# The weight and table preparation of a two-stage transformer kernel moved into its first attention stage

## What is computed

```python
dist = jnp.clip(seq[None, :] - seq[:, None], -MAX_POS, MAX_POS) + MAX_POS
attn = jax.nn.softmax(dots + conv[:, dist][None], axis=-1)
```

## Time and profile before

| | us |
|---|---|
| median of 3 runs (lowest, highest) | 3166.3 (3165.73, 3174.5) |
| the profiled execution: its own time | 3165.4 |
| its span, first to last instruction | 3163.4 |
| PE busy, share of the span | 2896.4, 92% |
| DVE busy | 2419.2, 76% |
| ACT busy | 2144.4, 68% |
| POOL busy | 380.2, 12% |

### The profile page before, as it was taken

How to read it: one execution, slowest core, us unless ns; L and a number is a source line. 1 busy time by engine, 2 the same in 40 slices (tenths; PEclk the granted TensorE clock), 3 DMA queues, 4 the chain that set the end, 5 groups by cost and what they waited for, 6 DMA issues and landing times. The chain is left out here.

```text
span 3163.4 us, 49154 instructions
## 1 busy us (share of the span) xinstructions
PE 2896.4 (92%) x19007; PEld 1293.5 (41%) x19007; DVE 2419.2 (76%) x3075; ACT 2144.4 (68%) x2683; POOL 380.2 (12%) x322
## 2 busy tenths in 40 slices
PE   5699999999779999999999999999999999999994
PEld 4356656665433333333333333333333333333331
DVE  6655656565868888888888888888888888888843
ACT  1155656555447777777777777777777777777783
POOL 0000000000001111111101111111111110111114
PEclk9699999999979999999999999999999999999996
DMA  6000000004244434435444444443453544345202
GB/s 178 18 11 2 28 2 22 8 23 82 59 94 77 104 93 88 111 93 111 75 100 95 94 104 99 86 97 94 88 110 97 107 74 105 95 88 110 53 22 88
DMA packets 144399, 243.90 MB, mean 77 GB/s; under 512 B 56562, under 2 KB 92934, under 8 KB 140838
## 3 DMA queue, kind: packets, MB, share of 16 engines
q1 hardware_dynamic: 143590, 238.67, 34.0%
q10 hardware_dynamic: 576, 2.10, 0.2%
HBM read 163.82 MB, written 74.10 MB: 75 GB/s over the span
## 5 line engine op out<-in xcount | busy, mean ns | idle before, releaser
L1598 ACT ACTIVATE pt_b<-ps_max 128x1024 f32<-128x1024 f32 x1516 | 1491.7, 1025 | 364.5 <-PE ps_max L1469 360.5
L1623 DVE TENSOR_REDUCE mx_b<-ps_pair 128x2 f32<-128x1024 f32 (+1 forms) x989 | 1193.5, 1207 | 166.9 <-PE ps_pair L1455 158.7
L1504 PE MATMUL ps_ctx<-pt_b,vs 128*32 128x512 f32 x6144 | 820.6, 606 | 3.8 <-ACT c_b L1587 3.5
L1623 DVE TENSOR_REDUCE mx_b<-ps_misc 128x1 f32<-128x512 f32 x989 | 677.7, 685 | 144.0 <-PE ps_misc L1455 125.7
L1469 PE MATMUL ps_max<-qs,ks 50*128 50x512 f32 x3032 | 780.4, 436 | 1.3 <-ACT part L1555 0.9
L1455 PE MATMUL ps_pair<-ks,qs 48*128 48x512 f32 x1955 | 512.3, 458 | 84.8 <-DVE mx_b L1623 84.6
L1469 PEld LDWEIGHTS ps_max<-qs,ks 50*128 50x128 f32 x3032 | 353.2, 186 | 344.0 <-ACT pt_b L1598 254.0
L1455 PE MATMUL ps_misc<-ks,qs 48*128 48x512 f32 x989 | 441.8, 447 | 7.1 <-DVE mx_b L1623 0.3
L960 ACT ACTIVATE pt<-ps_max,cb 128x512 f32<-128x512 f32 x340 | 215.0, 686 | 223.3 <-PE ps_max L801 159.5
L1455 PEld LDWEIGHTS ps_pair<-ks,qs 48*128 48x128 f32 x1955 | 207.4, 184 | 364.8 <-DVE mx_b L1623 332.5
L1455 PEld LDWEIGHTS ps_misc<-ks,qs 48*128 48x128 f32 x989 | 183.2, 185 | 333.4 <-DVE mx_b L1623 260.7
(11 more groups left out here) (194 smaller groups left out, 2257.6 us busy)
## 6 DMA issues: line engine op xcount, KB each, us to landing
partd<-part SPq DMA_DIRECT2D x22, 2048.0 KB, 9.1
qs<-partd SPq DMA_DIRECT2D x288, 128.0 KB, 5.6
ks<-partd SPq DMA_DIRECT2D x288, 128.0 KB, 6.7
xv<-node SPq DMA_DIRECT2D x26, 512.0 KB, 5.5
xf<-node SPq DMA_DIRECT2D x24, 512.0 KB, 4.7
node<-nt_b SPq DMA_DIRECT2D x48, 256.0 KB, 2.1
rec_b<-invd SPq DMA_DIRECT2D x368, 32.0 KB, 1.8
xq<-node SPq DMA_DIRECT2D x22, 512.0 KB, 3.8
```

What stands on the lines that cost most here:

```text
L1504: ins = pe.matmul(psO[SLOT * i:SLOT * i + SLOT, :], vs[u % 2][:, kb, QUAD * (s // HALF_STEPS) + i], pt[:, (QUAD * S + i) % ENTRIES], start ...
L1598: act.activation(pt[:, e:e + 2].rearrange("p k n -> p (k n)"), at[:], ACT.Exp, scale=SCALE_B).then_inc(exp_done, 1)
L1623: nc.vector.tensor_reduce(mx2[:, at:at + n], (psP, psX)[p % 2][:, 0:CHUNK * n].rearrange("p (h n) -> p h n", h=n), AX.X, ALU.max).then_inc ...
```

## The change

The block `prelude` and the HBM tensor `xnt` are gone, and their work stands in `first_attention`.

- **Tables.** `ext` has six rows: high parts for scores (0, 1) and maxima (2, 3), low parts for scores (4, 5), split by DVE on the 8 partitions of `extended()` before they are written. 32 DMAs read them straight into `tabM` and `tabS`. The products with `flip` are gone: `eye`, the stationary matrix of the window products, is built from the exchange matrix instead of the identity. The eight DMAs for the maxima of heads 0 to 3 go first, the other 24 after the loads of the fold's weights.
- **Layer norm.** Batch 0 is loaded to `xu`, normalised there (`next_stats`, `next_norm`) and turned into `xnb`. Batch b+1 is loaded during batch b, with statistics at step 4 of half 2b, `root_next` at step 6, the norm at step 8, and four transpositions each at steps 10 and 12 (`rows_turned`, `next_turned`). Loading it waits for the earlier rows to be turned.
- **Fold.** PE's part is cut in 13 pieces that follow the maxima p = 4, 6, ..., 28 of half 0; the copies and scalings run on ACT instead of DVE. All its tiles lie in storage that half 0 needs later (`pt`, `cn`, `c32`, `vs[1]`, `x1`, `nt`, `rec`, `den`), so ACT waits for `w_out_s` (results landed in HBM) before the first exponential. The three result DMAs are issued ahead of `rows_load(1)` and of the first `mr<-mhl`.
- **Setup.** Memsets move from DVE to POOL, the constants `cm` from before the projections to after the last maximum of half 0; `wo` and `bo` are waited for only before the first score.

The diff, cut to its core:

```diff
-    xnt = dram("xnt", [BATCH, P, TOK])
...
-    ext = dram("ext", [4, HEADS, NE])
+    ext = dram("ext", [EXT_ROWS, HEADS, NE])
...
-def prelude(nc, psM, psS, psX, sid, exchange, x_rows, conv, conv_rev, ew, act_w, We, be, Wq, Wk, Wv, Wo, ident,
...
+        weights = [within(cn[:], 4 * P * c, [4, P]) for c in range(4)] + [within(c32[:], 4 * P * c, [4, P]) for c in range(2)]
...
+        wos = within(vs[1][:], 0, [NODES, P])
+        wps, wvs, wfs = (within(pt[:], at, shape) for at, shape in (
+            (0, [NODES, WP_COLS]), (NODES * WP_COLS, [NODES, P]), (NODES * (WP_COLS + P), [NODES, WF_COLS])))
...
+        dv_ = within(pt[:], 0, [2, NE])[0:HEADS]
+        de = [within(pt[:], 2 * NE * (k + 1), [2, NE])[0:HEADS] for k in range(2)]
+        dhi = within(units.ks[1][:], 0, [4, NE])[0:HEADS]
+        dlo = within(units.qs[1][:], 0, [2, NE])[0:HEADS]
...
+                sp.dma_start(cv[:, 1], conv).then_inc(cv_in, D16)
+                sp.dma_start(cv[:, 0], conv_rev).then_inc(cv_in, D16)
+                sp.dma_start(xu[:], x_rows[0]).then_inc(xs_in, D16)
+                sp.dma_start(sid[:], ident).then_inc(id_in, D16)
+                sp.dma_start(exch, exchange).then_inc(id_in, D16)
                 sp.dma_start(wqk[:], w_qk).then_inc(w_in, D16)
...
+                                src = bass.AP(ext.tensor, ((2 + s) * HEADS + QUAD * q + odd) * NE + first + DQK * (1 - b),
+                                              [[1, DQK], [2 * NE, 2], [1, WIN]])
+                                sp.dma_start(tabM[rows, q, s, b].bitcast(F32), src).then_inc((tab_first, tab_in)[q], D16)
+
+                sp.wait_ge(ext_high, 1)
+                ext_write(dhi[:, 2:4].bitcast(F32), 2, ext_m_out)
...
+                sp.wait_ge(ext_m_out, D16)
+                maxima_tables(0)
...
+                sp.wait_ge(ext_low, 1)
+                ext_write(dhi[:, 0:2].bitcast(F32), 0, ext_out)
+                ext_write(dlo.bitcast(F32), 4, ext_out)
+                sp.wait_ge(ext_out, 2 * D16)
+                sp.wait_ge(xt_ready, 1)
+                for t, at, first, n, step in edge_loads:
+                    sp.dma_start(within(t, P * at, [n, P]), We[first:first + step * (n - 1) + 1:step].rearrange("e p n -> p e n")
+                                 ).then_inc(we_in, D16)
+                for k, w in enumerate((Wq, Wk, Wv, Wo)):
+                    for t, first, n in ((cn[:], 0, 4), (c32[:], 4, 2)):
+                        sp.dma_start(within(t, 0, [n, 4, P])[:, :, k], w[first:first + n].rearrange("c p n -> p c n")
+                                     ).then_inc(we_in, D16)
+                for q in range(2):
+                    for i in range(QUAD):
+                        rows = Wo[:, (QUAD * q + i) * DV:(QUAD * q + i + 1) * DV, :]
+                        at = SLOT * i + DV * q
+                        sp.dma_start(wos[at:at + DV], rows.rearrange("c d n -> d c n")).then_inc(wos_in, D16)
...
+                            for b in range(2):
+                                rows = slice(DQK * odd, DQK * odd + DQK)
+                                src = bass.AP(ext.tensor, ((4 * part_ + s) * HEADS + odd) * NE + first + DQK * (1 - b),
+                                              [[1, DQK], [2 * NE, HEADS // 2], [1, WIN]])
+                                sp.dma_start(tabS[rows, part_, s, b].bitcast(F32), src).then_inc(tab_in, D16)
+                maxima_tables(1)
...
+                sp.wait_ge(wo_ready, NODES)
+                sp.dma_start(wpd.rearrange("c p n -> p c n"), wps).then_inc(w_out_s, D16)
+                sp.dma_start(wvd.rearrange("c p n -> p c n"), wvs).then_inc(w_out_s, D16)
+                sp.dma_start(wfd.rearrange("c p n -> p c n"), wfs).then_inc(w_out_s, D16)
...
+
+                    sp.wait_ge(xt_ready, 2 * b - 1)
+                    sp.dma_start(xu[:], x_rows[b]).then_inc(xs_in, D16)
...
-                    if b < BATCH - 1:
-                        sp.wait_ge(v_ready, 2 * b + 2)
-                        sp.dma_start(xnb[:], xnt[b + 1]).then_inc(xn_in, D16)
...
+                def rows_turned(b, c):
+
+                    if not c:
+                        pe.wait_ge(ln_ready, b + 1)
+                    for t in range(BPC):
+                        ins = pe.transpose(psX[:, P * t:P * t + P], xu[:, P * (BPC * c + t):P * (BPC * c + t) + P], sid[:])
+                    ins.then_inc(xt_ready, 1)
+
+                def fold_turn(c):
+
+                    if not c:
+                        pe.wait_ge(scale_in, 3 * D16)
+                        pe.wait_ge(we_in, (5 + 8) * D16)
+                        pe.transpose(psO[:, 3 * P:3 * P + EDGE], ber[0:EDGE], sid[0:EDGE, 0:EDGE])
+                    else:
+                        pe.wait_ge(wt_copied, c)
+                    for k in range(3):
+                        ins = pe.transpose(psO[:, P * k:P * k + P], edge[EDGES[c][k]], sid[:])
+                    ins.then_inc(wt_ready, 1)
...
+                def fold_products(c):
+                    if c:
+                        pe.wait_ge(wo_ready, c)
+                    else:
+                        pe.wait_ge(be_copied, 1)
+                        pe.wait_ge(v_copied, 1)
+                    pe.wait_ge(wt_copied, c + 1)
+                    for k in range(3):
+                        pe.matmul(psX[:, P * k:P * k + P], wet[:, k], weights[c][:, k], start=True, stop=True)
+                    for k in range(3):
+                        ins = pe.matmul(psX[:, 3 * P + k:3 * P + k + 1], weights[c][:, k], bet[:, EDGES[c][k]:EDGES[c][k] + 1],
+                                        start=True, stop=True)
+                    ins.then_inc(wm_ready, 1)
...
+                def fold_bias(c):
+                    pe.wait_ge(wm_copied, c + 1)
+                    pe.matmul(psX[:, 3 * P + 4:3 * P + 5], weights[c][:, 3], bcol[:, 0:1], start=True, stop=True
+                              ).then_inc(wb_ready, 1)
...
+                            elif normed_next(hh):
+                                pe.wait_ge(xt_copied, 2 * normed_next(hh) + 1)
...
+                pe.wait_ge(id_in, 2 * D16)
+                pe.wait_ge(ln_ready, 1)
+                for t in range(KB):
+                    ins = pe.transpose(psM[0][:, P * t:P * t + P], xu[:, P * t:P * t + P], sid[:])
+                ins.then_inc(xt_ready, 1)
+                pe.wait_ge(w_in, 2 * D16)
                 for n in range(PJ_A):
                     project(0, n)
                 values(0)
+                pe.wait_ge(eye_done, 1)
+                pe.wait_ge(tab_first, 8 * D16)
                 for p in range(PIECES):
                     maxima(0, p)
-                pe.wait_ge(v_copied, 1)
+                    if p in FOLD_AT:
+                        fold(FOLD_AT[p])
+                pe.wait_ge(wo_ready, NODES)
                 turn_maxima(0)
                 pe.wait_ge(padded, 2)
+                pe.wait_ge(filled_in, 2)
+                pe.wait_ge(tab_in, 24 * D16)
+                pe.wait_ge(wo_a_in, (1 + 2 * QUAD) * D16)
...
+                def root_next(b):
+                    act.wait_ge(ln_ve_ready, b + 1)
+                    act.activation(ln_sd[:], ln_mv[:, :, 1], ACT.Sqrt).then_inc(ln_sd_ready, 1)
...
+                        act.wait_ge(wos_in, 2 * QUAD * D16)
+                        act.wait_ge(wt_ready, 1)
+                        act.activation(bet[:], psO[:, 3 * P:3 * P + EDGE], ACT.Identity).then_inc(be_copied, 1)
+                        act.wait_ge(be_copied, 1)
+                        act.wait_ge(ext_out, 2 * D16)
+                    act.wait_ge(wt_ready, c + 1)
+                    if c:
+                        act.wait_ge(wm_ready, c)
+                    act.activation(wet.rearrange("p k n -> p (k n)"), psO[:, 0:3 * P], ACT.Identity).then_inc(wt_copied, 1)
+                    act.activation(wfs[:, c, 0:P], edge[EDGES[c][0]], ACT.Identity, scale=s[0])
+                    act.activation(wfs[:, c, P:2 * P], wos[:, c], ACT.Identity, scale=aw)
+                    if c:
+                        act.wait_ge(wo_ready, c)
+                    act.activation(bsum[:], bet[:, EDGES[c][0]:EDGES[c][0] + 1], ACT.Identity, scale=s[0]).then_inc(wb_made, 1)
+                    act.wait_ge(wm_ready, c + 1)
+                    for k in range(2):
+                        act.activation(wps[:, c, P * k:P * k + P], psX[:, P * k:P * k + P], ACT.Identity, scale=s[k])
+                        act.activation(wps[:, c, 2 * P + k:2 * P + k + 1], psX[:, 3 * P + k:3 * P + k + 1], ACT.Identity,
+                                       scale=s[k])
+                    act.activation(wvs[:, c], psX[:, 2 * P:3 * P], ACT.Identity, scale=s[2])
+                    if c:
+                        act.wait_ge(wb_ready, c)
+                    act.activation(bcol[:], psX[:, 3 * P + 2:3 * P + 3], ACT.Identity, scale=s[2]).then_inc(wm_copied, 1)
...
+                def fold_bias(c):
+                    act.wait_ge(wb_ready, c + 1)
```

(71 more changed lines are left out.)

378 lines of the change are left out of this document (126 added, 252 removed).

## The result

The changed kernel takes 3097.52 us in the median (3096.45 to 3098.32, four runs) against 3166.02 (3164.01 to 3174.5, four runs) for the kernel before: a ratio of 0.9778, 95% interval 0.9760 to 0.9796. The prediction was 3108 us, range 3092 to 3128. The profiled execution took 3096.45 us with a span of 3094.2, 69.2 less than before.

What follows compares the result with a forecast made beforehand. PE was taken to bound the attention from the first score on, a chain without overlap the part before. 3165.4 - 66 (first score from 160.1 to 94 us) + 9 (halves) = 3108 us, range 3092 to 3128.

Steps and rivals of the forecast that it cites:

- Steps 1 to 3: Start of the kernel: batch 0 turned at 19 us, projections until 30.6, first maxima's tables there at 22.3, covered.
- Step 4: Start of the fold: it waits for weight and Wo loads, first products at 40.8 us, DVE dry some 4 us.
- Rival 2: Weight loads are the bound: Wo lands 12 us later, first score at 106, 3120 us in all; 15%.
- Step 5: Fold among the maxima: PE at the low clock bounds, 7.3 us a node, last node done at 82.2 us.
- Rival 1: The fold raises PE's clock to 2.4 GHz: 5.4 us a node, first score at 83, 3097 us; 17%.
- Step 6: DMA queue behind the fold: results out at 82.5, landed at 91.5, batch 1 behind them, first score at 94 us.
- Step 7: Layer norms inserted in halves 0, 2 and 4: 3 us a batch, 9 us lost, bounds 3.6 and 15.

Runs made afterwards that it cites:

- run 1: Changed kernel with the 13 fold pieces put behind the last maximum of half 0 instead of among the maxima: 3126.32 us.
- run 3: Changed kernel with one unread product of 128 rows and 512 columns ahead of each maximum of half 0: 3092.32 us.
- run 5: Changed kernel with each transposition of rows inside halves 0, 2 and 4 issued twice: 3093.77 us, on another chip.
- run 7: Changed kernel with the constants `cm` computed ahead of maximum 16 instead of behind the last: 3101.31 us, on another chip.
- run 10: Changed kernel with `cm` among the maxima, fold results sent in three parts, later wait for Wo, exponential's table loaded early: 3092.34 us, ratio to before 0.9771.
- run 12: Changed kernel with DVE normalising only the first of eight blocks of 128 tokens for batches 1 to 3: 3096.64 us.
- run 6: Changed kernel with the square root of batches 1 to 3 replaced by the identity: 3093.76 us, on another chip.
- run 8: Changed kernel with the eight table DMAs for the maxima of heads 4 to 7 issued twice: 3099.61 us, on another chip.
- run 11: The four edits of run 10 on the changed kernel, plus the extra unread products of run 3: 3091.48 us, ratio to before 0.9764.
- run 9: The changed kernel again, unaltered, five rounds against the kernel before: 3097.4 us, ratio 0.9775.

## Why the prediction was right, and by how much it was off

The signs and places were right: 3108 forecast, 3097.5 measured, inside the range. Most of the 10.5 us has a place. Against the profiled execution of before, 3165.4: -72.0, +6.1, -0.6 and -2.6 make 3096.3, where the profiled execution took 3096.45.

- **Steps 1 to 3** held within 0.5 us: copy 18.95 (19 forecast), first reduction 30.14 (30.6), the first tables issued from 10.1 to 16.7 and landing 5.5 us after issue in the median (7.6 is over all 16), so at 22 as forecast, before use.
- **Step 4, the weights, was mis-sized:** first products at 36.17, not 40.8. Each weight load cost SP 0.47 to 0.54 us of issue (one 0.80), not the 0.67 of the table DMAs, and landed in 3.4 to 5.2, not 7.9 us: the 7.9 was that of a 384 KB load with others before it in the queue. The 5 us that the step gives the Wo loads to land have no row behind them; they took 3.4. PE's first turn waited for nothing, and DVE's forecast gap of 4 us did not come. Rival 2 fell. The Trainium skill ("DMA: Bandwidth & Descriptors", Bandwidth, Measured) gave 138 GB/s for 64 KB, and the estimate from it had the weights last until 44 us. Its figure is for loads issued from GpSimd. Here the 21 loads of 48 to 384 KB, issued by SP with tables beside them, moved 191 to 220 GB/s in all (first two stretches), so that page's figure for 64 KB was no price for them; they also hold 2.9 MB, not the 3.2 of the prediction.
- **Step 5, the bound, was right:** PE at 1.2 GHz, busy 39.98 of 40.1, a node 7.06 us for 7.3, and run 1 and run 3 confirm it from both sides. With the earlier start the results went out at 76.7 for 82.5. But what the prediction took as settled, the clock, is not: over the same code the node period was 7.06 us at the low clock and 4.4 to 4.5 at the high one, with DVE as the bound (run 5), and where the high clock lasted or returned, the first score came up to 8 us earlier (80.01 in run 5, 88.15 in the first profile). Rival 1 (17%), which priced a node at 5.4, is what happens in part of a stage in some executions, by no edit of that stage. (The prediction counts a third of the fold as transpositions; by time they are 0.9 of the 4.0 us of a node.)
- **Step 6, the queue:** 11.5 us from the issue of the results to the first score forecast, 11.45 measured, and the agreement is partly luck. The prediction let the queue end last (94) and the chain 0.9 earlier (93.1). Measured, the chain ended last: the maxima's row took 4.13 us from issue to score, as behind a free queue, and the chain was 0.5 us longer than forecast. The queue was close behind, as run 7 shows; in run 10, where it was emptied early, the shorter chain is gained.
- **Step 7, the halves, was too dear:** 9 us forecast, 6.1 measured. Of the three terms a batch, 1.2 for transpositions measured 0.9 (run 5); two DVE blocks of 0.6 measured 0.7 for the norm (run 12) and no visible wait for the statistics; 0.6 for table loads and root was wrong in its premise: halves 2 and 4 get no loads that weren't there before, and in half 0, which gets two, leaving them out gave 0.1 us (run 6). 0.9 + 0.7 leaves 0.1 to 0.2 of the 1.77 us of halves 2 and 4. Half 0 costs 0.8 more; 0.3 of it lies in its first four projections (3.46 against 3.19 us before), where the clock rises, and about 0.3 in the norm, which costs 1.0 there (run 12); the rest is open. A half is 83.6 to 90.4 us, not the 91 of this step, whose window held some of the graph.
- **The graph:** the prediction had it unchanged; it took 2.6 us less. Over the fourteen profiled executions, whose code is the same there, graph and finish took 2281.0 to 2287.5 us. The graph starts at half clock in all of them, for 13 to 34 us, and in most the clock falls again later, for 3 to 14 us at a time. Added up over the first 2200 us behind the last rows, half clock lasts 24 us in run 10 (2280.95) and 45 us in run 8 (2287.5), 37 in run 11 (2285.52). Time and half clock go together (correlation 0.90, some 0.3 us for each us at half clock), with exceptions of up to 2 us: the first profile and run 9 both have 29 us, and 2281.7 and 2284.8. No run set the clock there, so this is a relation and no shown cause, and why the clock falls again stays open.

**How far the best version is better.** The medians of runs 10 and 11 lie 5.1 and 5.9 us under that of run 9 on the same chip, but the ratios' intervals overlap, and run 9 had one execution of 3085.04. The gain is likely, not shown. And the 4.7 us that the extra products gain ahead of the first score did not reach the end in the profiled pair.

## What to carry to other kernels

Mixing a stage bound by one engine (DVE, 36 us) with one bound by another or by latency (the fold, 36 us) cost 51 us in place of 72; price such a mix as the work of the busier engine, summed over both, at the clock it will really have, read from durations, not from the clock column alone. Before you shorten the chain behind a stage, ask what stands in the DMA queue beside it: two chains that tie hide each other's gain, as the constants showed. For inserted work, count per engine only what the slots can't hold: of 4.6 us of DVE work a batch 0.7 to 1.0 mattered, and of 2.8 us of ACT work in half 0 about 0.1, while the 0.9 of PE work counted whole. And look in the trace whether an edit took away what it was meant to: leaving out the root removed table loads in one half of three.

## What the runs showed of the hardware

- **The clock of a full PE.** PE was busy 39.98 of 40.10 us in a mix of 64-row maxima, windows, one-column products and transpositions, and stayed at 1.2 GHz all that time; with one more 128-row product of 512 columns a maximum it stayed at 2.4 (run 3, and again run 11). The Trainium skill ("TensorE: Matmul & The Clock Gate", Part 4) says that transpositions don't count as activity for the high clock. They are 0.9 of the 7 us of a node here, so this mix neither confirms nor refutes it.
- **It differs from execution to execution.** In nine executions in which PE's code of the stage is the same, the clock fell to 1.2 GHz between 33 and 41 us, and in two of them it rose again inside the stage, at 45.8 us (run 5) and at 59.8 and 70.1 us (run 8). The first score, with the code ahead of it unchanged, moved from 88.15 to 80.01.
- **Small DMAs behind large ones.** The four DMAs of 8 KB cost 2.50 us of issue and 4.04 us to the score with a queue that had emptied (before, and run 10). Behind 1.9 MB of results and 0.5 MB of rows it depended on how long before them the first of these had been issued: 4.04 to 4.62 us when it was 7.0 to 7.3 us (eight executions, 4.13 in the kernel after), 5.77 when it was 6.2 (run 7), and 8.70, with 3.99 of issue, when it was 3.8 (run 1).
- **Roots that share a table.** A square root directly behind another needed no table load: 0.19 us at 303.80, where one alone between exponentials cost two loads of 1.28 (130.49 to 133.29).
